# Regrouping the last layer's router, its coefficients and GpSimd's last weight passes in a four-layer transformer kernel

## The reference, cut to what matters

```python
x = x + tanh(g_xattn[0]) * L0_xattn(layernorm(x), ctx)      # fp8 product
x = x + tanh(g_ffn[0])   * L0_ffn(layernorm(x))             # 8 experts, dense, plus a shared one
x = x + tanh(g_xattn[1]) * L1_xattn(layernorm(x), ctx, ctx) # 16 heads, causal, 4 sequences
x = x + tanh(g_ffn[1])   * L1_ffn(layernorm(x))
# L1_ffn:
logits = gelu(x @ rw1) @ rw2                # rw1 256x128, rw2 128x8: the router
wgt, idx = top_k(softmax(logits), 2)
for e in range(8):
    Ye = gelu(x @ w1[e] + b1[e]) @ w2[e] + b2[e]     # hidden size 1024
    Ce = gelu(b1[e]) @ w2[e] + b2[e]                 # output of expert e for a token not sent to it
    for k in range(2):
        mask = idx[..., k] == e
        active = any(mask)
        out += active * wgt[..., k:k+1] * where(mask, Ye, Ce)
```

## Time and profile before

| what | us |
|---|---|
| three runs | 415.46, 412.56, 414.46 |
| median | 414.46 |
| profiled execution, its own time | 415.43 |
| its span, first to last instruction | 413.7 |
| PE busy in the span | 316.0 (76%) |
| DVE busy | 301.4 (73%) |
| ACT busy | 261.3 (63%) |
| POOL busy | 162.9 (39%) |

### The profile page before, as it was taken

How to read it: one execution, slowest core, us unless ns; L and a number is a source line. 1 busy time by engine, 2 the same in 40 slices (tenths; PEclk the granted TensorE clock), 3 DMA queues, 4 the chain that set the end, 5 groups by cost and what they waited for, 6 DMA issues and landing times.

```text
span 413.7 us, 8523 instructions
## 1 busy us (share of the span) xinstructions
PE 316.0 (76%) x2638; PEld 215.3 (52%) x2639; DVE 301.4 (73%) x729; ACT 261.3 (63%) x528; POOL 162.9 (39%) x219
## 2 busy tenths in 40 slices
PE   0073988999999967687583511879999999999981
PEld 0062326764577545354241310756777777777750
DVE  4998998665862747759676886874777778887760
ACT  1845757634865575948778796331777777777770
POOL 4051300083483360613661358500445444444432
PEclk9997898999999979879778665886999999999997
DMA  6974000033283173311313576442777677777522
GB/s 201 392 235 141 1 0 2 1 101 103 71 227 115 41 202 93 104 51 53 103 52 103 182 229 229 167 169 100 246 253 244 210 228 249 232 254 253 152 28 27
DMA packets 28098, 60.44 MB, mean 146 GB/s; under 512 B 4401, under 2 KB 19010, under 8 KB 24866
## 3 DMA queue, kind: packets, MB, share of 16 engines
q1 hardware_dynamic: 21186, 52.64, 36.8%
q0 software_dynamic: 4416, 6.13, 9.2%
q10 hardware_dynamic: 2464, 1.27, 1.2%
HBM read 27.43 MB, written 6.32 MB: 82 GB/s over the span
## 4 chain that ended last, share of the span: by engine, by line
PE 39%; DVE 29%; issue 13%; ACT 10%; POOL 4%; DMA 3%; ACTq 1%; DVEq 0%; POOLq 0%
PE bank L1226 7%; PE bank L1586 6%; PE bank L1568 5%; DVE MX L1926 4%; ACT arena L1087 3%; PE bank L1589 3%; PE bank L1571 3%; PE bank L1187 3%; POOL arena L681 2%; DVE arena L2196 2%; ACT arena L1094 2%; DVE arena L2191 2%; PE bank L1304 1%; PE bank L1324 1%; ACT arena L969 1%
## 5 line engine op out<-in xcount | busy, mean ns | idle before, releaser
L1087 ACT ACTIVATE arena<-arena,B1D 128x128 f32<-128x128 f32 x184 | 57.3, 392 | 14.6 <-DVE arena L2191 14.1
L1586 PE MATMUL bank<-arena 128*128 x184 | 63.4, 390 | 1.1 <-DVE arena L2196 1.1
L2191 DVE TENSOR_REDUCE arena<-bank 128x256 f32<-128x512 f32 x92 | 57.1, 680 | 0.9 <-PE bank L1571 0.9
L681 POOL TENSOR_TENSOR arena<-STG,arena 128x256 f16<-128x256 f32 x52 | 37.1, 747 | 44.8 <-ACT arena L859 41.0
L1589 PE MATMUL bank<-arena 128*128 x184 | 51.3, 279 | 0.0
L754 POOL DMA_INDIRECT out_dram<-arena,SI x23 | 37.2, 1616 | 31.6 <-DMA out_dram<-arena,SI 24.4
L681 POOL TENSOR_TENSOR W<-STG,W 128x256 f16<-128x256 f32 x56 | 36.0, 682 | 33.6 <-ACT W L859 28.6
L2196 DVE SCALAR_TENSOR_TENSOR arena<-arena 128x512 f16<-128x512 f32 x46 | 29.7, 688 | 24.9 <-ACT arena L1094 24.9
L741 POOL DMA_INDIRECT arena<-token_rows,GI x23 | 24.4, 1062 | 58.1 <-ACT WS L1081 48.6
L1568 PE MATMUL bank<-arena 128*128 128x256 f16 x256 | 45.6, 279 | 1.1 <-issue 0.6
L1571 PE MATMUL bank<-arena 128*128 128x128 f16 x256 | 44.6, 223 | 0.0
(11 more groups left out here) (271 smaller groups left out, 700.9 us busy)
## 6 DMA issues: line engine op xcount, KB each, us to landing
arena<-W SPq DMA_DIRECT2D x16, 1024.0 KB, 4.7
STG<-in_l_w_dram SPq DMA_DIRECT2D x30, 512.0 KB, 4.1
STG<-W SPq DMA_DIRECT2D x7, 1024.0 KB, 5.4
arena<-in_l_w_dram SPq DMA_DIRECT2D x2, 1280.0 KB, 8.7
X<-in_x_dram SPq DMA_DIRECT2D x2, 512.0 KB, 3.6
W<-in_ctx_t_dram ACTq DMA_DIRECT2D x2, 512.0 KB, 6.0
W<-in_ctx_dram SPq DMA_DIRECT2D x1, 1024.0 KB, 13.3
k_parts<-W SPq DMA_DIRECT2D x2, 512.0 KB, 3.3
```

The source lines that it names most:

```text
L681: ins = nc.gpsimd.tensor_tensor(l, src, h, ALU.subtract)
L1087: ins = nc.scalar.activation(x, x, ACT.Gelu, bias=B1D[:, e, c:c + 1], scale=1.0 / (X_SCALE * W_SCALE))
L1586: nc.tensor.matmul(bank[6 + q][:, :], GDL[:, q, 0, c * P:(c + 1) * P], W2[:, e, c].rearrange("p s d -> p (s d)"), start=(c == 0), stop=Fal ...
L2191: v.tensor_reduce(half, o, AX.X, ALU.add).then_inc(s_dadd, 1)
```

## The change

It does six things. One weight block moves from after the attention into the up passes of the first feed-forward layer (block 5 joins block 4 there; all later blocks move up by one, so `D_BLOCKS` begins at 22), and in the first sequence of the attention the middle block is scaled at step 5 and no longer at step 4. The router runs in three groups of tiles: 0 to 3, 4 and 5, and 6 and 7. The first two groups need no tile of the last two, so their product, gelu and logits stand before the last rows' layernorm is finished; DVE's split of the first group stands between its last variance and the last scaled rows. ACT's gelu of b1 moves ahead of the router's gelus. DVE's coefficients move from behind the copy of tile 0's rows to just behind the row list. `fold_groups` moves from the first turn of the tile loop to the second, behind its up pass. POOL keeps block 24 before the list and does blocks 25 to 28 behind gathers 0 and 1 (25 and 26 before gather 2, 27 and 28 before gather 3); block 29 becomes a third late block for DVE, while only 30 and 31 (`APART`) have buffers of their own. POOL's low pass of the first block of `D_BLOCKS` moves ahead of the last `estimate_rstd`, and DVE does one block where it did three.

```diff
-        C_BLOCKS = [range(10, 13), range(13, 16), range(16, 19), range(19, 21)]
-        SCALE_AT = ((1, 4, 8), (2, 5, 8), (2, 5, 8), (2, 5))
-        D_BLOCKS = range(21, BLOCKS)
-        VECTOR_BLOCKS = D_BLOCKS[1:4]
-        LATE_BLOCKS = D_BLOCKS[-2:]
+        C_BLOCKS = [range(11, 14), range(14, 17), range(17, 20), range(20, 22)]
+        SCALE_AT = ((1, 5, 8), (2, 5, 8), (2, 5, 8), (2, 5))
+        D_BLOCKS = range(22, BLOCKS)
+        LATE_BLOCKS = D_BLOCKS[-3:]
+        APART = D_BLOCKS[-2:]
+        GROUPS_R = ((range(0, 4), bank[3], 0), (range(4, 6), bank[2], 0), (range(6, 8), bank[4], 0))
...
 # SP
-            for i in LATE_BLOCKS:
+            for i in APART:
                 load_weights(i)
-            for i in range(28, LATE_BLOCKS[0]):
+            for i in range(28, APART[0]):
                 load_weights(i)
...
-            sp.wait_ge(s_wlo, BLOCKS - 2)
+            sp.wait_ge(s_wlo, LATE_BLOCKS[0])
+            sp.wait_ge(s_wlate, 3)
             load_tile_weights(2, 2, first=True)
...
 # POOL
-            weights_low(4)
+            for i in range(4, 6):
+                weights_low(i)
             pool.wait_ge(s_up, 2 * CA)
...
             weights_low(C_BLOCKS[3][1])
+            weights_low(D_BLOCKS[0])
             estimate_rstd(11, 3, 2)
-            weights_low(D_BLOCKS[0])
...
-            pool.wait_ge(s_wlo, VECTOR_BLOCKS[-1] + 1)
-            weights_low(D_BLOCKS[4])
-            pool.wait_ge(s_eid, 1)
-            for i in D_BLOCKS[5:7]:
-                weights_low(i)
+            pool.wait_ge(s_wlo, D_BLOCKS[2])
+            weights_low(D_BLOCKS[2])
...
             for j in range(4):
-                if j == 2:
-                    for i in D_BLOCKS[7:-2]:
+                if j >= 2:
+                    for i in D_BLOCKS[2 * j - 1:2 * j + 1]:
                         weights_low(i)
                 gather_rows(j)
...
 # ACT
             hidden_gelu(CA + 5)
+            weights_scale(4)
             hidden_gelu(CA + 6)
+            weights_high(4)
             hidden_gelu(CA + 7)
-            weights_scale(4)
+            weights_scale(5)
             hidden_gelu(CA + 8)
-            weights_high(4)
+            weights_high(5)
...
+            weights_split(D_BLOCKS[0])
+            rows_t_out(2)
+            nc.scalar.activation(GB[:, :, :], B1D[:, :, :], ACT.Gelu).then_inc(s_gb, 1)
+            router_gelu(0)
+            router_gelu(1)
+            weights_split(D_BLOCKS[1])
+            for t in (6, 7):
+                row_high(t)
+            weights_scale(D_BLOCKS[2])
+            rows_t_out(3)
+            weights_high(D_BLOCKS[2])
+            router_gelu(2)
...
 # PE
+            transpose_rows(2)
+            router_product(0)
+            router_product(1)
+            router_logits(0)
+            router_logits(1).then_inc(s_dlg, 1)
+            transpose_rows(3)
+            router_product(2)
+            router_logits(2).then_inc(s_dlg, 1)
...
                 if n:
                     pe.wait_ge(s_gb16, 2)
-                    pe.wait_ge(s_wlo, BLOCKS - 2)
-                else:
-                    pe.wait_ge(s_wlate, 2)
+                    pe.wait_ge(s_wlo, LATE_BLOCKS[0])
+                    pe.wait_ge(s_wlate, 3)
...
                 tile_up(j, j % 2, j % 3, j // 3, first=j == 0)
+                if j == 1:
+                    fold_groups()
                 transpose_tile(j + 1, (j + 1) % 2, (j + 1) // 2)
                 if j == 0:
                     transpose_coefficients()
                     idle_outputs(1)
                     idle_outputs(0)
-                    fold_groups()
...
 # DVE
             ln_variance(3, 11, 2)
+            split_router(0)
             scaled_rows(3)
-            for t in range(HT, T):
+            split_router(1)
+            for t in (6, 7):
                 row_low(t)
+            i = D_BLOCKS[1]
+            v.tensor_tensor(weight_block(i)[2], staged(i), weight_block(i)[1], ALU.subtract).then_inc(s_wlo, 1)
+            choices(0, range(0, 6))
+            split_router(2)
+            choices(1, range(6, 8))
...
             step(v.tensor_scalar(ACTV[...], bank[3][:, 0:2 * E], 0.0, None, ALU.is_gt))
-            late_low(LATE_BLOCKS[0])
+            chosen = DTOPF[:, :, :].unsqueeze(3).broadcast_to([P, T, 2, E])
+            ... # SLOTM, CF, IDLE and COEF, as they stood behind rows_t(0)
+            late_low(APART[0])
             dve.wait_ge(s_gb, 1)
...
             rows_t(0, 0, first=True)
-            ... # SLOTM, CF, IDLE and COEF
-            late_low(LATE_BLOCKS[1])
...
             for j in range(HEAD):
                 add_halves(j, j % 2, first=j < 2)
+                if j == 1:
+                    folded_out()
                 rows_t(j + 1, (j + 1) % 2, first=j == 0)
+                if j == 0:
+                    late_low(APART[1])
+                    late_low(LATE_BLOCKS[0])
+                    coefficients_out()
+                if j == 1:
+                    add_idle_shares()
                 for hb in range(2):
                     split_hidden(j, j % 2, hb)
                 if j == 0:
                     idle_outputs_out()
-                if j == 1:
-                    add_idle_shares()
```

More of the change, by code:

```diff
@@ L532, in _ @@
             load_k_stack(0)
-            for i in range(4, 9):
+            for i in range(4, 10):
                 load_weights(i)
@@ L544, in _ @@
             load_k_stack(2)
-            for i in range(14, 16):
+            for i in range(15, 17):
                 load_weights(i)
@@ L1009, in _ @@
                 q_high(1, i)
-            for i in range(5, 10):
+            for i in range(6, 11):
                 weights_split(i)
@@ new lines, in choices @@
+            def choices(n, tiles):
+                dve.wait_ge(s_dlg, n + 1)
+                for t in tiles:
+                    mark(v.max(DTOP[:, t], logit_of(t)))
+                here()
+                ts = slice(tiles[0], tiles[-1] + 1)
+                rows = (bank[6][:, 0:6 * E] if n == 0 else bank[5][:, S + 6 * E:S + 8 * E]).rearrange("p (t e) -> p t e", e=E)
+                v.tensor_tensor(GAP[:, ts, 0:E], rows, DTOP[:, ts, 0:1].broadcast_to([P, len(tiles), E]),
+                                ALU.subtract).then_inc(s_dl, 1)
+                if n:
+                    v.tensor_tensor(GAP[:, :, E], DTOP[:, :, 1], DTOP[:, :, 0], ALU.subtract).then_inc(s_dl, 1)
+                for t in tiles:
+                    mark(v.max_index(DTOPI[:, t], DTOP[:, t], logit_of(t)))
+                here()
```

136 lines of the change are left out of this document (61 added, 75 removed).

## The result

The changed kernel takes 417.40 us (median of 5 runs, 416.28 to 417.60) against 413.99 us for the kernel before (median of 5 runs, the three above and two more): ratio 1.0077, 95% interval 1.0047 to 1.0107. The change makes the kernel 0.8% slower, under the 1% that the prediction takes as the bound between same and slower, and the time is 1.4 us under the 418.8 us predicted. The profiled execution took 417.6 us, its span 415.9 us; before 415.43 and 413.7.

A forecast was written before the change was run, and what follows sets the result against it. A chain of waits across engines before the PE-bound tile loop was taken to set the time; 1.5 - 7.0 + 11.4 - 1.6 = +4.3 us on 414.46 gave 418.8 us, range 413.5 to 424.

The forecast's parts named there:

- The case that was held likeliest: Whole kernel: block 29 gates the first up pass, half clock only partly in idle outputs; 418.8 us, 416.5 to 421.5, chance 0.50.
- the ungated rival: Row list to third up pass: block 29's load leaves before the list, rows' copy waits only for its gather; 408.8 us, chance 0.08.
- The signs that were named: Trace around the row list: DVE idle some 8 us, first up matmul about 17 us behind list, PE gap before idle outputs.
- part 3: Row list to first up matmul: a chain through block 29 takes 17.3 us against 5.9, +11.4 us (+10.9 to +12.0).
- part 4: First to third up pass: 25.6 us against 27.2, first down pass at full clock; -1.6 us (-3.7 to +2.5).
- Part 1: Stages before the last variance: the weight block moved to earlier stages costs +1.5 us (0 to 2.2).
- The first place: Block 4's low pass on POOL beside DVE's four rstd steps: 0.62 us each, delaying PE's third score product; +1.1 us.
- part 2: Last variance to row list: choice marks 4.3 us sooner, slots 2.7 us shorter; -7.0 us (-6.3 to -8.0).
- the second place: Attention's first sequence: block scaled at step 5 behind ACT's wait, +0.7 us, less 0.3 for DVE's next low half.
- two outcomes, 17.8 and 16.9: Row list to first up matmul: 17.8 us if coefficients beside gather 0 keep it near 1.87, 16.9 if they don't.
- The clock holds: Idle outputs: PE's gap is too short to lower the clock, they take 3.68 us; -2.1 us, 416.7 us, chance 0.24.
- The clock stays low: Idle outputs through first down pass: clock at half throughout; +4.1 us, 422.9 us, chance 0.18.

The follow-up runs named there:

- after: The changed kernel itself, 417.40 us; run once more unedited beside later experiments, 418.25 us, ratio 1.0138 to the kernel before.
- the first experiment: The changed kernel with POOL's low pass of block 25 moved from behind gathers 0 and 1 to in front of the row list: 408.47 us, ratio 0.9908.
- the fold's experiment: The kernel before with fold behind the second up pass, coefficients' copies ahead of tile 0's split, shares added ahead of tile 1's split: 409.07 us.
- the moved block alone: The kernel before with only the one weight block moved to the earlier stages, later blocks one place earlier: 412.89 us, ratio 1.0013.
- The warm products: The changed kernel with 28 dense products, result unused, between the coefficients' transposes and the idle outputs: 419.38 us, ratio 1.0180.
- the coefficients behind: The changed kernel with the coefficients, all but the first step, back behind the copy of tile 0's rows: 418.10 us, ratio 1.0147.
- no gate: The changed kernel with POOL's block 25 before the list, 26 to 28 before gather 2, DVE's late passes 29, 30 before the copy, 31 behind: 406.98 us; again 407.30.

## Why the prediction was right, and where its terms were off

The sum was +4.3 us for the end; the two profiled executions differ by 2.2, the medians by 3.4, and by 4.6 when after ran once more. The case that was held likeliest came, but for the first down pass, and block 29 gates the start, which the first experiment shows by removing it: 408.47 us, where the ungated rival was priced at 408.8. The signs that were named came too: DVE's wait before the late pass of block 30 (11.93 us), a gap of PE ahead of the idle outputs, the first up matmul 16.16 us behind the list. Of the chances that it gave, slower had 0.49 and same 0.44; 0.8% is just on the side of same. That the sum comes as near as it does is in part luck: part 3 was 1.2 us too high and part 4 1.3 too low.

**Part 1 (+1.5 predicted).** The first place is borne out, though the table's +0.05 hides it. The rstd steps took 0.47 to 0.60 us each, and PE's third score product, 105.95 in the earlier trace rows, came at 106.54 in a profile that was 0.75 us ahead at the variance before it, so 1.34 late, where 1.1 was taken. The slip is still there at the next variance: 30.22 us from 94.36 to 124.58, 29.08 in before. The +0.05 is the sum of that +1.14, of the 0.75 by which this profile was ahead at its start, of +0.68 that belongs to part 2, and of 1.0 won in the attention (49.33 us between the variances around it, 50.34 in before), where before's profile had the lower granted clock. That 1.0 is luck of the draw: the fold's experiment, with before's program, has 48.24 there. What the second place costs (0.4 in the sum) is not settled, nor is the whole part by times (+0.5, -1.1 to +2.2, for the moved block alone).

**Part 2 (-7.0, in two terms of 4.3 and 2.7).** Right: -4.78 and -2.55, -7.33 from the last variance on. Of the first, 1.77 is shown by putting POOL's pass back beside DVE's steps; the other 3.0 (12.26 against 15.27, the pass behind in both) belong to the regrouped router and the orders around it together, and no run takes these apart. The second is shown whole, +2.55 with POOL's blocks back beside the slots. A price was left out: ahead of the variance the last scaling of the attention's output lies beside the pass now, 0.52 and 0.77 us for its last two instructions where before shows 0.42 and 0.48, and 0.52 for a small step that took 0.23. From the variance before it to the last one after takes 16.71 and before 16.03, +0.68.

**Part 3 (17.3 us from list to first up matmul).** 16.16. Every link was there in the order given; three were sized too high. Block 29's load landed in 3.47 us, not the 4.2 of the earlier trace rows; from the end of the late pass to the first matmul it is 1.17 us, where 1.6 was taken; and from the list to POOL's block 25 it is 3.42 (3.6 taken, with gather 0 between 0.97 and 1.87; it took 1.22). The other links: 2.56 for the block (2.55), 4.28 on ACT with the hand-over (4.2), 1.22 for the late pass.

The Trainium skill's rule ("SBUF — State Buffer", "SBUF: two separate sides": GpSimd has to write its descriptors, and VectorE work that holds their shared port shuts it out) was given two outcomes, 17.8 and 16.9; it came to 16.16, below both. The trace doesn't show the lock-out for these small operations: gather 0 takes 1.22 us with the coefficients beside it and 1.22 without. Beside a late pass it took 1.87, which fits one.

**Part 4 (25.6 us from first to third up pass).** 26.86, so -0.31 instead of -1.6. The term that failed is the first down pass at full clock, 2.65. The gap ahead of the idle outputs was taken as 3.5 us and is 2.04, mostly since up 0 and the transposes took 6.75 and not 5.7 (the clock, at half behind PE's wait, rose only near 268, when up 0 was done, and in before near 262, within it); the idle outputs became ready 8.79 us behind the first up matmul (9.2 taken) and took 5.34 (5.8), so the shares began 18.55 behind it and ended at 22.6, about as forecast (22.9). Then the clock fell a second time and the down pass took 4.29. The reason that I gave for full clock, the vanished stall in the shares, is refuted by the fold's experiment: no stall, half clock. The earlier trace rows had been misread, too: its stretch, 276 to 278, lies over the stall (up to 277.49) and not behind it.

**The clock rivals.** "The clock holds" priced 2.1 us for a clock that stays up in the idle outputs. The warm products made just that happen, and the third up pass didn't move. In the profile with the coefficients behind the copy, too, the idle outputs ran 3.68 us at full clock behind a gap of 3.21, and the first down pass took 5.09. But the gain can also be kept. From the start of the idle outputs to the third up pass after takes 18.07 us, the warm products 18.15, the coefficients behind 17.64; with block 25 ahead it is 16.53, and with no gate 16.36 in one profile and 17.92 in the other. So the rival's price of 2.1 is not what a held clock gives: in these profiles it is 1.7 or almost nothing, and the same program gave both. "The clock stays low" didn't come whole: between the two places the clock was at 1.00; but its half clock in the first down pass did come.

**Where the expected gain went.** 7.3 us of it, 6.7 net of what the pass costs ahead of the variance, is real and sits ahead of the row list. It was turned into a new wait behind the list, because the block whose buffer the last load needs was put behind something that waits for the list. With that one block back in front the change is worth 0.9% (408.47 us), and with the late passes ordered so that the second gate opens too 1.3% (406.98 us). The second step alone isn't told apart by the times, whose intervals overlap; from the list to the third up pass it is 32.11 us with the first and 30.40 and 31.38 with both.

## What to carry to other kernels

When work is moved behind a wait, follow each buffer that it frees: the load into that buffer, and everything queued behind that load on every engine, moves with it; here one 2.6 us pass held a chain of 16 us. Where two engines slow each other, undoing the order is a cheap test; price both ends of it, since a pass that leaves one place (-1.77 us) lies in another (+0.67). And compare stage lengths between fixed marks, not absolute times: up to the first up matmul they repeat within 0.2 us where whole runs wander by several. Where a stage does wander, one profile on each side decides nothing; take a second profile of the same program first.

## What the runs showed of the hardware that was not expected

- The granted clock falls to half while PE is busy 2.00 us of 2.00 (the fold's experiment). In all the profiles of this study it falls within the shares or soon behind, and the first down pass takes 3.9 to 5.1 us, where the next one takes 2.60 at full clock in after. The length of an idle time ahead of thin products does not decide it: a gap of 2.04 us went with half clock (after), gaps of 2.38 (block 25 ahead) and 3.21 (coefficients behind) did not; and the stall among the shares went with half clock in before (0.52 from 276 to 278) and with full clock in the kernel with the moved block alone (2.10 us, 1.00 from 276 to 278). Dense products among the thin ones did not keep it up, and with +7.4 us for work reckoned at 1.8 us filler products were a poor means here. What sets the fall stays open.
- Two-operand passes of DVE and POOL beside each other slow both, by up to two thirds: two blocks on POOL take 5.05 us with DVE at work on other things, 8.37 with DVE's late passes and splits beside them, and a DVE pass of 1.22 then takes 1.5 to 1.7. Small steps are stretched more: 0.15 to 0.62.
- Without a late pass beside it the first gather takes 1.22 us, with DVE idle or busy with small steps, and the second 0.97. Beside a late pass the first takes 1.87 to 1.99 (the three profiles that have before's order there) and the second 1.37 (no gate). What makes the first one longer when nothing lies beside it was not tried.
- The way to the last variance differs by 6 us between profiles of kernels that hardly differ there, and by 3.3 us between two of the same program up to there. The granted clock between 150 and 160 us is 0.67 in some and 0.83 in others; in the two of the same program the lower clock goes with the longer way through the attention (50.34 and 48.24 us between the variances around it). What sets that clock was not found.
